# The attention stage of a graph network rewritten: one wide sum per tile, copied out by ScalarE, scaled in place, with rows shared with GpSimd

## The chip, the cores and the metric

One Trainium2 chip, one core of it. The metric is the device time of one execution in microseconds (us), shown as the median of several runs. Engines go by the names of the profile: PE is TensorE, DVE is VectorE, ACT is ScalarE, POOL is GpSimd, SP is SyncE.

## The reference, cut to what matters

The network has 50,000 nodes and 50,000 edges, 64 features, and four layers on a residual stream. The layer that is changed here is the third, a GATv2 attention with 4 heads over the edges and one loop per node:

```python
m = leaky_relu(x_l[src] + x_r[dst] + e_emb, 0.2)
alpha = einsum('ehf,hf->eh', m, att)
amax = segment_max(alpha, dst)
ex = exp(alpha - amax[dst])
denom = segment_sum(ex, dst)
alpha = ex / (denom[dst] + 1e-16)
out = segment_sum(x_l[src] * alpha[..., None], dst).mean(axis=1) + bias
out = gamma * (out - out.mean(axis=0)) * rsqrt(out.var(axis=0) + 1e-5) + beta   # then relu
```

The edges are sorted by `dst`.

## The kernel before, in words

`kernel()` builds a row of stages, each an `nc.Block()` in which every engine has its own instruction list and the engines meet through semaphores alone. In order of time: preparation, two norm layers, the attention's edge scores and segment maximum, the stage `attention("fa")` (line 2465) that is changed, `batch_norm("fb")` (line 2740), three typed layers. A stage starts when the one before has ended on all engines.

**The attention stage** has the scores of every edge and loop ready: the exponentials in the table `exp_all` (8 numbers per edge: 4 exponentials and 4 maxima, one per head), the maxima of the loops in `amax`. It makes the weighted sums of source rows. It goes over the nodes in NS = 56 blocks of HS = 7 tiles of 128 nodes. For a block it loads a window of WT = 8 tiles of edge rows (`win`), their 8 numbers into the last 8 columns of `M`, and the nodes' own rows (`own`). All buffers that matter are double (slot n % 2). Per block, before the change:

- DVE `matrices` (line 2643): one comparison makes `S`, 14 selection matrices of 128x128 (each of the 7 node tiles looks at BAND = 2 edge tiles).
- DVE `messages` (2650): `M[:, :, 0:256]` = edge row times exponential, 4 heads, one instruction of 2048 elements.
- PE `small_sums` (2534): 14 matmuls of 8 columns (sum of exponentials, maximum) into bank 7.
- DVE `differences` and `weights` (2657, 2669): small operations and an exponential by ACT (`exps`, 2596) give two factors per node and head: `cc[:, 0]` for the edges' sum and `cc[:, 1]` for the loop.
- PE `sums` (2545): 14 matmuls of 256 columns, two node tiles to a bank, banks 0 to 3.
- ACT `own_edges` (2600): `mine` = own row times `cc[:, 1]` for 4 of the 7 tiles, 16 instructions. DVE does the other 3 tiles at the top of `scale` (2690).
- DVE `scale` (2690): 28 instructions of 64 columns (tile by head): sum in the bank times `cc[:, 0]` plus `mine`, to `agg`. Each pair of tiles raises `scaled`, which frees its bank.
- PE `turns` (2557): 14 transposes of `agg`; ACT `turned` copies them to `aggT` in 4 pieces; PE `outputs` (2573): the product with the output weights, 64 output partitions, 512 and 384 columns into banks 5 and 6; ACT `outputs` (2617) copies it with the bias to `oT`; SP stores it; DVE `moments` (2679) takes the statistics for the batch norm, two instructions of 448 columns.

The order on PE is sums(n), turns(n-1), small_sums(n+1), outputs(n-1); on DVE matrices(n+1), messages(n+1), moments(n-2), scale(n), differences(n+1), weights(n+1); on ACT own_edges(n), turned(n-1), exps(n+1), outputs(n-1). POOL has nothing in this stage. Each f32 matmul stands in the trace as two weight loads and two matmuls. At the end `bn_aggr` (2726) joins all statistics and a few small operations make the batch norm's factors.

The other lines that the prediction names: 2259, 2260 and 2262 are the sums of the second norm layer, where 2259 writes the bank's partitions 64 to 127 and the other two the partitions 0 to 63; 2783 is a POOL product of the batch norm stage and 2838 a DVE operation beside it; 261 and 1790 are POOL index fills of the preparing stages.

Of the kernel before, what the change touches and what calls it, by code (L numbers as in the profile page):

```python
# [4 lines left out]
P = 128  # L5
F = 64
HEADS = 4
HF = HEADS * F
HS = 7
# [4 lines left out]
WT = HS + 1  # L14
# [4 lines left out]
BAND = 2  # L19
# [8 lines left out]
def build_gnn(nc, a, out):  # L28
# [47 lines left out]
    with ctx:  # L76
# [2388 lines left out]
        def attention(tag):  # L2465
            with nc.cleanup_on_exit(), ExitStack() as c, nc.Block() as block:
# [17 lines left out]
                small = carve(early, [P, HS, E8]); me = carve(early, [P, HS, HEADS]); mm = carve(early, [P, HS, HEADS])  # L2484
# [3 lines left out]
                mine = tb("mine", [P, HS, HEADS, F]); agg = tb("agg", [P, 2, HS, HEADS, F])  # L2488
                aggT = tb("aggT", [P, 2, HS * P]); oT = tb("oT", [F, HS * P])
                stats = tb("stats", [F, 2 * NS, 6]); mv = tb("mv", [F, 4])  # L2490
                win_in, ex_in, own_in = two("win_in"), two("ex_in"), two("own_in")
                (S_ok, M_ok, small_ok, small_read, d_ok, e_ok, c_ok, mine_ok, sums_ok, scaled, aT_made, aT_read, out_made, o_ok, stat_ok, stored, var_ok, sd_ok) = (
                    sm(n) for n in ("S_ok", "M_ok", "small_ok", "small_read", "d_ok", "e_ok", "c_ok", "mine_ok", "sums_ok", "scaled", "aT_made", "aT_read", "out_made",
                                    "o_ok", "stat_ok", "stored", "var_ok", "sd_ok"))
                CH = [(0, 4), (4, HS)]
                PAIRS = [(t, min(t + 2, HS)) for t in range(0, HS, 2)]
                NB = len(PAIRS)
                TURNS = [(0, 0, 4), (0, 1, 5), (1, 0, 6), (1, 1, 4)]
                small_ps = bank[7][:, 0:HS * E8].rearrange("p (t c) -> p t c", c=E8)
                assert N > (NS - 1) * HS * P  # L2500

                @block.sync
                def _(sp):
                    def load(n):
# [3 lines left out]
                        if n >= 2:  # L2508
                            sp.wait_ge(M_ok, n - 1)
                        sp.dma_start(win[:, s, :, :], tiles(edge_all[bass.ds(begin, WR), :])).then_inc(win_in[s], 16)  # L2510
                        if n >= 2:
                            sp.wait_ge(sums_ok, NB * (n - 1))
                        sp.dma_start(M[:, s, :, HF:MW], tiles(exp_all[bass.ds(begin, WR), :])).then_inc(ex_in[s], 16)
                        if n >= 2:
                            sp.wait_ge(scaled, NB * (n - 1))
                        sp.dma_start(own[:, s, :, :], tiles(node_g[at, :])).then_inc(own_in[s], 16)

                    def store(n):
                        sp.wait_ge(o_ok, 2 * n + 2)
                        sp.dma_start(gat_rows[:, n * HS * P:(n + 1) * HS * P], oT[:, :]).then_inc(stored, 16)  # L2520
# [9 lines left out]
                    sp.wait_ge(stored, 16 * NS)  # L2530

                @block.tensor
                def _(pe):
                    def small_sums(n):
                        s = n % 2
                        pe.wait_ge(S_ok, n + 1)
                        pe.wait_ge(ex_in[s], 16 * (n // 2 + 1))
                        if n >= 1:
                            pe.wait_ge(small_read, n)
                        for t in range(HS):  # L2540
                            for q in range(BAND):
                                ins = nc.tensor.matmul(small_ps[:, t, :], S[:, s, BAND * t + q, :], M[:, s, t + q, HF:MW], start=(q == 0), stop=(q == BAND - 1))
                        ins.then_inc(small_ok, 1)

                    def sums(n):
                        s = n % 2
                        pe.wait_ge(M_ok, n + 1)
                        for b, (t0, t1) in enumerate(PAIRS):
                            if n >= 1:
                                pe.wait_ge(scaled, NB * (n - 1) + b + 1)  # L2550
                            for t in range(t0, t1):
                                for q in range(BAND):
                                    ins = nc.tensor.matmul(bank[b][:, (t - t0) * HF:(t - t0 + 1) * HF], S[:, s, BAND * t + q, :], M[:, s, t + q, 0:HF],  # L2553
                                                           start=(q == 0), stop=(q == BAND - 1))
                            ins.then_inc(sums_ok, 1)

                    def turns(n):
                        s = n % 2
                        pe.wait_ge(scaled, NB * (n + 1))
                        for k, (b, q, to) in enumerate(TURNS):  # L2560
                            if k == 3:
                                pe.wait_ge(aT_read, 4 * n + 1)
                            elif n >= 1:
                                if k == 0:
                                    pe.wait_ge(aT_read, 4 * n)
                                else:
                                    pe.wait_ge(o_ok, 2 * (n - 1) + k)
                            t0, t1 = CH[b]
                            for t in range(t0, t1):
                                ins = nc.tensor.transpose(bank[to][:, (t - t0) * P:(t - t0 + 1) * P], agg[:, s, t, 2 * q:2 * q + 2, :].rearrange("p h f -> p (h f)"), ident[:, :])  # L2570
                            ins.then_inc(aT_made, 1)

                    def outputs(n):
                        for b, (t0, t1) in enumerate(CH):
                            pe.wait_ge(aT_read, 4 * n + 2 * b + 2)
                            for q in range(2):
# [350 lines left out]
```

## Time and profile before

| | |
|---|---|
| median of 3 runs | 5102.17 us (5100.82 to 5104.14) |
| the profiled execution's own time | 5098.76 us |
| its span | 5096.6 us |
| PE busy | 4014.7 us (79%) |
| PE weight loads busy | 3596.6 us (71%) |
| DVE busy | 3622.2 us (71%) |
| ACT busy | 2008.4 us (39%) |
| POOL busy | 2562.4 us (50%) |

How to read it: busy times are of the whole span and mix stages with different limits; the attention stage is 2511 to 3341 us. What lies around the span (5098.76 - 5096.6 = 2.2 us) belongs to the launch.

### The profile page before, as it was taken

Reading aid. Unit: us, or ns where it says so; the run is one execution under the profiler, and the core shown is the slowest. Engines: PE = TensorE matmul, PEld = TensorE weight load, DVE = VectorE, ACT = ScalarE, POOL = GpSimd, SP = SyncE. Lnnn points to the kernel's source line nnn. Section 1 sums busy time; section 2 is a strip of 40 time slices with the busy share of each in tenths; the row PEclk is TensorE's granted clock in tenths of the full one; section 3 lists DMA queues with packets and bytes.
Section 4 is the critical chain, followed back from the end, with each engine's and each line's share of the span. In section 5 each row is a group of like instructions: output and inputs, shape, how many; then the busy total and the mean of one; then the engine's idle time right before and its main releaser. Section 6 shows DMA issues by size and latency. Waiting matters only on the chain. (4 is left out here: it accounts for less than half of the span.)

```text
span 5096.6 us, 86759 instructions
## 1 busy us (share of the span) xinstructions
PE 4014.7 (79%) x26962; PEld 3596.6 (71%) x27018; DVE 3622.2 (71%) x9781; ACT 2008.4 (39%) x4938; POOL 2562.4 (50%) x2806
## 2 busy tenths in 40 slices
PE   5710577658887999999399999996888688878888
PEld 5710577658776777777377777786888688877888
DVE  8977577857776999999699999976444344434554
ACT  6836244434444444444154444554222122222222
POOL 0010777747775777776000000035777577757775
PEclk9965777778988999999699999955898888888888
DMA  8013688857775544454122222245666466655665
GB/s 220 6 37 80 144 184 187 189 114 162 160 158 120 119 114 118 115 118 106 32 54 54 52 53 52 52 117 126 133 138 135 105 134 135 137 110 127 136 133 114
DMA packets 1642253, 583.15 MB, mean 114 GB/s; under 512 B 1548519, under 2 KB 1574950, under 8 KB 1641578
## 3 DMA queue, kind: packets, MB, share of 16 engines
q1 hardware_dynamic: 921158, 297.65, 26.1%
q10 hardware_dynamic: 636612, 195.74, 16.5%
q0 software_dynamic: 84064, 84.64, 8.2%
q8 instruction: 205, 3.36, 0.3%
q14 instruction: 214, 1.75, 0.1%
HBM read 381.77 MB, written 209.21 MB: 116 GB/s over the span
## 5 line engine op out<-in xcount | busy, mean ns | idle before, releaser
L2001 POOL DMA_INDIRECT early<-node_g,src_w x1173 | 1115.5, 951 | 427.0 <-issue 356.8
L2218 POOL DMA_INDIRECT early<-node_g,src_w x782 | 758.6, 970 | 297.7 <-issue 249.0
L2783 POOL TENSOR_TENSOR fbt_c<-x_sb,fbln 128x128 f32<-128x128 f32 x56 | 22.4, 400 | 1022.4 <-DVE fbln L2859 1022.4
L1116 POOL DMA_INDIRECT fscat<-node_g,early x392 | 371.7, 948 | 192.9 <-issue 110.5
L2262 PE MATMUL bank<-l0S,l0msg 128*128 128x128 f32 x1568 | 272.6, 353 | 158.0 <-issue 69.2
L1220 ACT ACTIVATE fsy<-bank 128x512 f32<-128x512 f32 x448 | 240.1, 544 | 379.1 <-DVE fslz L1265 201.3
L2262 PEld LDWEIGHTS bank<-l0S,l0msg 128*128 128x128 f32 x1568 | 262.4, 265 | 164.8 <-issue 120.0
L2553 PE MATMUL bank<-early,faS 128*128 128x256 f32 x1568 | 358.0, 386 | 0.0
L2553 PEld LDWEIGHTS bank<-early,faS 128*128 128x128 f32 x1568 | 296.6, 192 | 73.3 <-issue 34.4
L2043 PE MATMUL bank<-l3S,l3msg 128*128 128x128 f32 x1568 | 234.5, 319 | 100.3 <-issue 60.8
L2043 PE MATMUL bank<-l5S,l5msg 128*128 128x128 f32 x1568 | 231.1, 316 | 100.3 <-issue 65.5
L2705 DVE SCALAR_TENSOR_TENSOR faagg<-bank,early,famine 128x64 f32<-128x64 f32 x1568 | 305.7, 275 | 5.7 <-ACT famine L2606 1.6
L2043 PE MATMUL bank<-l4S,l4msg 128*128 128x128 f32 x1568 | 234.6, 320 | 93.0 <-issue 59.3
L2043 PEld LDWEIGHTS bank<-l3S,l3msg 128*128 128x128 f32 x1568 | 225.8, 233 | 104.3 <-issue 104.3
L2043 PEld LDWEIGHTS bank<-l5S,l5msg 128*128 128x128 f32 x1568 | 222.5, 230 | 104.5 <-issue 104.5
L2043 PEld LDWEIGHTS bank<-l4S,l4msg 128*128 128x128 f32 x1568 | 225.8, 233 | 97.1 <-issue 97.1
L1265 DVE TENSOR_TENSOR fslz<-bank,fsy 128x512 f32<-128x512 f32 x448 | 258.3, 618 | 34.2 <-ACT fsy L1220 15.2
L2259 PE MATMUL bank<-ident,l1own 128*64 128x128 f32 x784 | 185.5, 334 | 122.0 <-issue 71.2
L2262 PE MATMUL bank<-l1S,l1msg 128*64 128x128 f32 x1568 | 270.2, 301 | 0.0
L2143 DVE TENSOR_TENSOR l3msg<-early,bank 128x512 f32<-128x512 f32 x112 | 71.9, 684 | 276.3 <-DMA early<-edge_h 276.1
L2143 DVE TENSOR_TENSOR l4msg<-early,bank 128x512 f32<-128x512 f32 x112 | 71.9, 684 | 274.9 <-DMA early<-edge_h 274.8
L1119 POOL DMA_INDIRECT fscat<-node_g,early x224 | 212.4, 948 | 68.3 <-issue 67.4
(365 smaller groups left out, 10920.6 us busy)
## 6 DMA issues: line engine op xcount, KB each, us to landing
edge_h<-early SPq DMA_DIRECT2D x280, 224.0 KB
node_g<-amax ACTq DMA_DIRECT2D x224, 224.0 KB
early<-edge_h SPq DMA_DIRECT2D x168, 256.0 KB
early<-node_g,src_w POOLq DMA_INDIRECT x1955
l0msg<-edge_a ACTq DMA_DIRECT2D x56, 256.0 KB
l0msg<-edge_h SPq DMA_DIRECT2D x56, 256.0 KB
l1msg<-edge_h SPq DMA_DIRECT2D x56, 256.0 KB
alpha<-edge_h SPq DMA_DIRECT2D x56, 256.0 KB
```

What stands on the lines that cost most here:

```text
L1116: pool.indirect_dma_start(out=cat[:, s, t, 0:F], out_offset=None, in_=node_g, in_offset=bass.IndirectOffsetOnAxis(ap=src_i[:, col], axis=0 ...
L1119: pool.indirect_dma_start(out=cat[:, s, t, F:2 * F], out_offset=None, in_=node_g, in_offset=bass.IndirectOffsetOnAxis(ap=dst_i[:, col], ax ...
L1220: A.activation(y[:, g % 2, 0:t1 - t0, :], z_bank(g)[:, 0:(t1 - t0) * HF].rearrange("p (t c) -> p t c", c=HF), ACT.Copy, scale=SLOPE).then_ ...
L1265: v.tensor_tensor(lz[:, kind, t0:t1, :], z_bank(g)[:, 0:(t1 - t0) * HF].rearrange("p (t c) -> p t c", c=HF), y[:, g % 2, 0:t1 - t0, :], AL ...
L2001: pool.indirect_dma_start(out=ring[:, n % RING, t, :], out_offset=None, in_=table_in, in_offset=bass.IndirectOffsetOnAxis(ap=src_w[:, n * ...
L2043: nc.tensor.matmul(to, msg[:, s, t + q, :], S[:, s, BAND * t + q, :], start=(q == 0), stop=(q == BAND - 1))
L2143: ins = v.tensor_tensor(msg[:, n % 2, :, r * F:(r + 1) * F], win[:, n % DEEP, :, :], rel_ps(n)[:, r, :].unsqueeze(2).to_broadcast((P, WT, ...
L2218: pool.indirect_dma_start(out=ring[:, n % RING, t, :], out_offset=None, in_=table_in, in_offset=bass.IndirectOffsetOnAxis(ap=src_w[:, n * ...
L2259: nc.tensor.matmul(bank[2 * s + b][F:2 * F, col], own[:, d, t, :], ident[:, :], start=True, stop=True)
L2262: ins = nc.tensor.matmul(to, msg[:, d, t + q, :], S[:, s, BAND * t + q, :], start=(q == 0 and conv), stop=(q == BAND - 1))
L2553: ins = nc.tensor.matmul(bank[b][:, (t - t0) * HF:(t - t0 + 1) * HF], S[:, s, BAND * t + q, :], M[:, s, t + q, 0:HF], start=(q == 0), stop ...
L2705: ins = v.scalar_tensor_tensor(agg[:, s, t, h, :], bank[b][:, lo:lo + F], cc[:, 0, t, h:h + 1], mine[:, t, h, :], ALU.mult, ALU.add)
```

## The change

All of it is inside `attention`:

- The separate small sums are gone. Each of the 14 matmuls now has 264 columns (256 of messages and 8 of exponentials and maxima). One tile has one bank, tile g uses bank g % 4.
- ACT copies each tile's 264 sums out of its bank into `agg` (`take`, 7 copies per block, semaphore `taken_ok`); a bank is free once its copy is done. `agg` now has 264 columns.
- DVE reads the small sums out of `agg`, waits for all 7 copies before `differences`, and runs `scale` as one in-place instruction of 1792 elements and `add` as two (3 tiles, 4 tiles).
- The own rows: ACT makes 3 tiles (OWN_ACT), POOL 4 in one instruction of 1024 elements. The messages: DVE makes 5 of the 8 edge tiles (MSG_DVE), POOL 3 in one instruction of 768 elements.
- The outputs go to both halves of one bank: columns 0 to 447 to partitions 0 to 63, columns 448 to 895 to partitions 64 to 127. ACT then has one copy per block, DVE one statistics instruction on 128 partitions, and `oT` is double.
- SP stores two halves per block. At the end it moves the upper half's statistics to the lower partitions with a DMA for which `bn_aggr` waits; at the start it loads `shift` (the bias, twice).
- New orders: matrices and messages run two blocks ahead; `outputs` lags two blocks and stands between the sums of tile 3 and tile 4.

The diff, cut to its core:

```diff
-                ACT_TILES = 4
+                OWN_ACT, MSG_DVE = 3, 5
...
                         if n >= 2:
                             sp.wait_ge(M_ok, n - 1)
+                            sp.wait_ge(M2_ok, n - 1)
                         sp.dma_start(win[:, s, :, :], tiles(edge_all[bass.ds(begin, WR), :])).then_inc(win_in[s], 16)
                         if n >= 2:
-                            sp.wait_ge(scaled, NB * (n - 1))
+                            sp.wait_ge(mine_ok, n - 1)
+                            sp.wait_ge(mine2_ok, n - 1)
                         sp.dma_start(own[:, s, :, :], tiles(node_g[at, :])).then_inc(own_in[s], 16)
...
+                    sp.wait_ge(stat_ok, NS)
+                    sp.dma_start(stats[0:F, NS:2 * NS, :], stats[F:2 * F, 0:NS, :]).then_inc(turned_stats, 16)
...
+                @block.gpsimd
+                def _(pool):
+                    def messages(n):
+                        s = n % 2
+                        pool.wait_ge(win_in[s], 16 * (n // 2 + 1))
+                        pool.wait_ge(ex_in[s], 16 * (n // 2 + 1))
+                        k = WT - MSG_DVE
+                        g.tensor_tensor(heads(M[:, s, MSG_DVE:WT, 0:HF]), win[:, s, MSG_DVE:WT, :].unsqueeze(2).to_broadcast((P, k, HEADS, F)),
+                                        M[:, s, MSG_DVE:WT, HF:HF + HEADS].unsqueeze(3).to_broadcast((P, k, HEADS, F)), ALU.mult).then_inc(M2_ok, 1)
+                    def own_edges(n):
+                        s, k = n % 2, HS - OWN_ACT
+                        pool.wait_ge(c_ok, n + 1)
+                        pool.wait_ge(own_in[s], 16 * (n // 2 + 1))
+                        g.tensor_tensor(mine[:, OWN_ACT:HS, :, :], own[:, s, OWN_ACT:HS, :].unsqueeze(2).to_broadcast((P, k, HEADS, F)),
+                                        cc[:, 1, OWN_ACT:HS, :].unsqueeze(3).to_broadcast((P, k, HEADS, F)), ALU.mult).then_inc(mine2_ok, 1)
+                    messages(0)
+                    messages(1)
+                    for n in range(NS):
+                        own_edges(n)
+                        if n + 2 < NS:
+                            messages(n + 2)
...
+                        for t in range(t0, t1):
+                            g = n * HS + t
+                            if g >= 4:
+                                pe.wait_ge(taken_ok, g - 3)
                             for q in range(BAND):
-                                ins = nc.tensor.matmul(small_ps[:, t, :], S[:, s, BAND * t + q, :], M[:, s, t + q, HF:MW], start=(q == 0), stop=(q == BAND - 1))
...
+                                ins = nc.tensor.matmul(bank[g % 4][:, 0:MW], S[:, s, BAND * t + q, :], M[:, s, t + q, :], start=(q == 0), stop=(q == BAND - 1))
...
+                        pe.wait_ge(aT_read, 4 * n + 4)
+                        if n >= 1:
+                            pe.wait_ge(o_ok, n)
+                        for q in range(2):
+                            for half in range(2):
+                                ins = nc.tensor.matmul(bank[7][half * F:(half + 1) * F, 0:HALF], Wst[:, q, :], aggT[:, q, half * HALF:(half + 1) * HALF], start=(q == 0), stop=(q == 1))
...
                     for n in range(NS):
-                        sums(n)
+                        sums(n, 0, SPLIT_AT)
+                        if n >= 2:
+                            outputs(n - 2)
+                        sums(n, SPLIT_AT, HS)
                         if n >= 1:
                             turns(n - 1)
...
+                            A.copy(agg[:, s, t, :], bank[g % 4][:, 0:MW]).then_inc(taken_ok, 1)
...
+                    for n in range(NS):
+                        take(n, 0, 2)
                         if n >= 1:
+                            own_edges(n - 1, 0, 1)
+                        take(n, 2, SPLIT_AT)
                         if n >= 1:
+                            own_edges(n - 1, 1, OWN_ACT)
+                        if n >= 2:
+                            outputs(n - 2)
+                        take(n, SPLIT_AT, HS)
                         if n >= 1:
+                            turned(n - 1, 0, 2)
+                        exps(n)
+                        if n >= 1:
+                            turned(n - 1, 2, 4)
...
                     def differences(n):
-                        dve.wait_ge(small_ok, n + 1)
-                        v.tensor_copy(small[:, :, :], small_ps).then_inc(small_read, 1)
+                        dve.wait_ge(taken_ok, HS * (n + 1))
...
                     def scale(n):
+                        v.tensor_tensor(heads(agg[:, s, :, 0:HF]), heads(agg[:, s, :, 0:HF]), cc[:, 0, :, :].unsqueeze(3).to_broadcast((P, HS, HEADS, F)), ALU.mult)
+                    def add(n):
+                        v.drain()
                         dve.wait_ge(mine_ok, n + 1)
+                        v.tensor_tensor(heads(agg[:, s, 0:OWN_ACT, 0:HF]), heads(agg[:, s, 0:OWN_ACT, 0:HF]), mine[:, 0:OWN_ACT, :, :], ALU.add)
+                        dve.wait_ge(mine2_ok, n + 1)
+                        v.tensor_tensor(heads(agg[:, s, OWN_ACT:HS, 0:HF]), heads(agg[:, s, OWN_ACT:HS, 0:HF]), mine[:, OWN_ACT:HS, :, :], ALU.add).then_inc(agg_ok, 1)
...
                     for n in range(NS):
+                        differences(n)
+                        if n + 2 < NS:
+                            matrices(n + 2)
+                        weights(n)
+                        scale(n)
+                        if n + 2 < NS:
+                            messages(n + 2)
+                        add(n)
                         if n >= 2:
                             moments(n - 2)
...
+                    dve.wait_ge(turned_stats, 16)
```

## Rows read from the trace of the kernel before

**Rows 1.** Stages: stretch, length, busy us of PE, PEld, DVE, ACT, POOL, clock, DMA.

```profile
515.00:1060.00 545.00, 370.43 (x2352) 355.77 (x2352) 401.49 (x1233) 235.43 (x616) 381.12 (x391) 0.75 0.74 172
2522.00:3334.00 812.00, 812.00 (x4342) 621.66 (x4342) 741.52 (x2348) 399.62 (x1287) 0.00 (x0) 0.97 0.26 51
3523.00:4045.00 522.00, 427.81 (x3360) 423.82 (x3360) 220.88 (x284) 113.86 (x224) 370.15 (x391) 0.87 0.58 128
```

**Rows 2.** Timeline: start, duration, engine, line. First and last of 56 `scale` groups on DVE.

```profile
2530.23 5.46 DVE L2705 SCALAR_TENSOR_TENSOR faagg<-bank,early,famine 128x64 f32<-128x64 f32 x28
...
3322.91 5.46 DVE L2705 SCALAR_TENSOR_TENSOR faagg<-bank,early,famine 128x64 f32<-128x64 f32 x28 [1.61 <-ACT famine L2606]
```

**Rows 3.** Timeline of PE over one block at full clock.

```profile
2542.09 1.82 PE L2570 MATMUL bank<-ident,faagg 128*128 128x128 f32 x14
2543.76 3.19 PE L2542 MATMUL bank<-early,faS 128*128 128x8 f32 x28
2546.88 3.22 PE L2577 MATMUL bank<-faaggT,Wst 128*64 128x512 f32 x8
2550.03 6.31 PE L2553 MATMUL bank<-early,faS 128*128 128x256 f32 x28
2556.17 1.82 PE L2570 MATMUL bank<-ident,faagg 128*128 128x128 f32 x14
```

**Rows 4.** Timeline of DVE and ACT over the same block.

```profile
2549.11 0.19 DVE L2662 TENSOR_TENSOR early<-early,no_edge 128x28 f32<-128x28 f32 x1
2549.74 0.18 DVE L2667 TENSOR_TENSOR early<-amax,early 128x28 f32<-128x28 f32 x1
2550.24 0.19 DVE L2671 TENSOR_TENSOR early<-early 128x28 f32<-128x28 f32 x1 [0.32 <-ACT early L2598]
2551.17 0.22 DVE L2677 TENSOR_TENSOR early<-early 128x56 f32<-128x56 f32 x1
2551.30 2.02 DVE L2647 TENSOR_TENSOR faS<-node_id,edge_id 128x1792 f32<-128x1792 f32 x1
2551.42 3.93 ACT L2606 ACTIVATE famine<-early 128x64 f32<-128x64 f32 x16 [0.18 <-DVE early L2677]
2555.44 1.14 DVE L2686 BATCH_NORM_STATS2 fastats<-faoT 64x6 f32<-64x448 f32 x2
2556.81 1.84 ACT L2615 COPY faaggT<-bank 128x512 f32<-128x512 f32 x4 [1.46 <-PE bank L2570]
```

**Rows 5.** Groups by line and shape in the attention stage: busy us, mean ns.

```profile
L2654 DVE TENSOR_TENSOR early<-alpha,early 128x2048 f32<-128x2048 f32 x56 | 127.9, 2284 | 2.8 <-DMA early<-edge_x 2.8
L2615 ACT COPY faaggT<-bank 128x512 f32<-128x512 f32 x112 | 60.2, 590 | 121.0 <-PE bank L2570 121.0
L2694 DVE TENSOR_TENSOR famine<-early 128x768 f32<-128x768 f32 x56 | 53.6, 958 | 9.8 <-issue 9.6
L2615 ACT COPY faaggT<-bank 128x384 f32<-128x384 f32 x112 | 49.3, 503 | 0.0
```

**Rows 6.** Groups of POOL over the whole span, by shape.

```profile
L2783 POOL TENSOR_TENSOR fbt_c<-x_sb,fbln 128x128 f32<-128x128 f32 x56 | 22.4, 400 | 1022.4 <-DVE fbln L2859 1022.4
L1790 POOL IOTA wn_tile_i<- 128x392 int32 x1 | 0.5, 455 | 84.1 <-ACTq L1774 84.1
L261 POOL IOTA row_i<- 128x128 int32 x1 | 0.2, 233 | 0.4 <-POOLq L2912 0.4
```

**Rows 7.** Timeline: DVE and POOL side by side in the batch norm stage.

```profile
3441.37 0.62 DVE L2838 SCALAR_TENSOR_TENSOR x_sb<-bank,x_sb 128x448 f32<-128x448 f32 x1
3441.49 0.40 POOL L2783 TENSOR_TENSOR fbt_c<-x_sb,fbln 128x128 f32<-128x128 f32 x1 [1.36 <-DVE fbln L2859]
```

**Rows 8.** Timeline of PE in the second norm layer, line 2259 of two neighbouring tiles.

```profile
1300.78 0.32 PE L2259 MATMUL bank<-ident,l1own 128*64 128x128 f32 x1
...
1301.43 0.32 PE L2259 MATMUL bank<-ident,l1own 128*64 128x128 f32 x1
```

**Rows 9.** DMA issues within the attention stage: KB each, median us to landing.

```profile
early<-edge_x SPq DMA_DIRECT2D x53, 32.0 KB, 2.2
```

More of the change, by code:

```diff
@@ L2487, in attention @@
                 S = tb("S", [P, 2, BAND * HS, P])
[L2488 to L2494, printed above, removed]
+                agg = tb("agg", [P, 2, HS, MW]); mine = tb("mine", [P, HS, HEADS, F])
@@ new lines, in attention @@
+                HALF = HS * P // 2
+                aggT = tb("aggT", [P, 2, HS * P]); oT = tb("oT", [P, 2, HALF]); shift = tb("shift", [P, 1])
+                stats = tb("stats", [P, 2 * NS, 6]); mv = tb("mv", [F, 4])
+                win_in, ex_in, own_in, stored = two("win_in"), two("ex_in"), two("own_in"), two("stored")
+                (shift_in, S_ok, M_ok, M2_ok, sums_ok, taken_ok, d_ok, e_ok, c_ok, mine_ok, mine2_ok, agg_ok, aT_made, aT_read, out_made, o_ok, stat_ok, turned_stats, var_ok, sd_ok) = (
+                    sm(n) for n in ("shift_in", "S_ok", "M_ok", "M2_ok", "sums_ok", "taken_ok", "d_ok", "e_ok", "c_ok", "mine_ok", "mine2_ok", "agg_ok", "aT_made", "aT_read", "out_made",
+                                    "o_ok", "stat_ok", "turned_stats", "var_ok", "sd_ok"))
@@ L2495, in attention @@
                 CH = [(0, 4), (4, HS)]
[L2496 to L2497 removed]
                 TURNS = [(0, 0, 4), (0, 1, 5), (1, 0, 6), (1, 1, 4)]
[L2499 to L2500 removed]
+                SPLIT_AT = 4
+                last_half = N - (NS - 1) * HS * P - HALF
+                assert 0 < last_half <= HALF
+                heads = lambda ap: ap.rearrange("p t (h f) -> p t h f", h=HEADS)
@@ L2545, in sums @@
[L2545 to L2554, printed above, removed]
+                        if t0 == 0:
+                            pe.wait_ge(S_ok, n + 1)
+                            pe.wait_ge(M_ok, n + 1)
+                            pe.wait_ge(M2_ok, n + 1)
@@ L2571, in turns @@
                             ins.then_inc(aT_made, 1)
                     def outputs(n):
-                        for b, (t0, t1) in enumerate(CH):
-                            pe.wait_ge(aT_read, 4 * n + 2 * b + 2)
-                            for q in range(2):
-                                ins = nc.tensor.matmul(bank[5 + b][0:F, 0:(t1 - t0) * P], Wst[:, q, :], aggT[:, q, t0 * P:t1 * P], start=(q == 0), stop=(q == 1))
-                            ins.then_inc(out_made, 1)
-                    small_sums(0)
+                        pe.wait_ge(aT_read, 4 * n + 4)
@@ L2708, in _ @@
                     matrices(0)
                     messages(0)
-                    differences(0)
-                    weights(0)
+                    matrices(1)
+                    messages(1)
                     for n in range(NS):
-                        if n + 1 < NS:
-                            matrices(n + 1)
-                            messages(n + 1)
+                        differences(n)
[6 more added lines that the diff above has]
+                        add(n)
```

140 lines of the change are left out of this document (61 added, 79 removed).

## The prediction

> **What bounds the kernel now.** I read the stages first [rows 1], the whole time second, the timeline of one block third. The attention stage runs from 2522 to 3334 us with PE busy all the time, DVE 741.5 of 812 us, ACT half, POOL not at all, at a mean clock of 0.97. The change touches this stage alone, so all the rest of the span should stay. The pace of the stage comes from the first and the last `scale` group: they start at 2530.23 and 3322.91, 55 blocks apart [rows 2], which is 792.68 / 55 = 14.41 us per block. Any answer is 55 or 56 times a difference to this number.
>
> Two engines come close to it. PE, from start to start in one block at full clock [rows 3]: transposes 2543.76 - 2542.09 = 1.67, small sums 3.12, outputs 3.15, sums 6.14, together 14.08 us. There is no gap between them, so PE is the limit at full clock; the rest up to 14.41 comes where the clock is lower for a moment. DVE is nearly as full: 741.5 / 812 x 14.41 = 13.2 us busy per block, and its drains fill most of what is left. A change that relieves only one of them wins nearly nothing. This one relieves both.
>
> **PE, part by part.** The small sums cost 3.12 us per block for 8 columns a matmul. They go; the 14 wide matmuls grow from 256 to 264 columns, 6.14 x 264 / 256 = 6.33 us. The transposes stay at 1.67. The outputs have the same columns (2 x 896) but are now pairs, one to each half of the partitions. What this is worth can be read elsewhere in this trace: the norm layer has per tile 4 matmuls of 128 columns in 8 records, two of which (line 2259) go to the upper half [rows 8]. From tile to tile 0.65 us pass (1300.78 to 1301.43). Eight records one after another at the pace of the sums here, 6.14 / 28 = 0.219 us for 256 columns or 0.11 for 128, would need 0.88; six need 0.66. So the upper half's records ran beside the others. I take the outputs at half, 3.15 / 2 = 1.6 us; the other end is 3.15. PE: 6.33 + 1.67 + 1.6 = 9.6 us at full clock, 11.15 if nothing overlaps.
>
> **DVE.** Two-operand operations cost 958 ns for 768 elements and 2284 for 2048 [rows 5], so 1.036 ns per element and 162 fixed. New per block: differences without the copy 2549.92 - 2549.11 = 0.81; matrices 2.02; weights 2551.39 - 2550.24 = 1.15 [rows 4]; scale, 1792 elements as the matrices have, 2.02, in place of 28 instructions in 5.46; messages for 5 tiles, 1280 elements, 1.49 instead of 2.28; add 0.96 (768) and 1.22 (1024); moments one instead of two instructions, 0.6, and its drain and semaphore 0.17. The own rows' 0.96 leave DVE. Sum 10.4; with four or five pauses of about 0.1 at drains and semaphores 10.9 us, against 14.3.
>
> **ACT.** It gets 7 copies of 264 columns. 512 columns take 590 ns and 384 take 503 [rows 5], 0.68 per column, so 0.42 each and 2.9 us. Own rows fall from 16 to 12 instructions of 3.93 / 16 = 0.245, 2.9 us; `turned` stays 1.84 [rows 4]; one output copy 0.6 and an exponential 0.25. Sum 8.6 us. It is not the limit, but its order matters: the own rows of block n wait for `c_ok` and then stand around the copies of tiles 2 and 3 of block n+1. From `c_ok` ACT needs 0.98 + 0.8 + 1.96 = 3.8 us to `mine_ok`; DVE meanwhile does scale and messages, 3.6 us. That wait costs DVE about 0.2. What is queued behind it is `add`, then `turns` on PE. The exponential of block n+1 stands behind two copies of turned rows; those are done 1.9 us after `add(n)`, while DVE is at matrices until 3.7 us. It costs nothing. If that cover went, it would cost 1 us at most.
>
> **POOL.** The nearest row is its product of 128 elements, 400 ns; its index fills give 233 ns for 128 and 455 for 392 elements, so 0.84 per element and 125 fixed [rows 6]. With the same fixed part the product costs (400 - 125) / 128 = 2.15 ns per element: own rows (1024) 2.33 us, messages (768) 1.78 us, sum 4.1 us per block. Bounds: 0.8 (both at 400 ns) and 5.6 (all of the 400 ns by element). The own rows are due when `add` begins its second part, 4.6 us after `c_ok`, the messages one block later: both ends are hidden, if the engines do not disturb each other.
>
> **Do they?** No row shows POOL and DVE in two-operand SBUF work at once. The nearest one has POOL's product inside a DVE operation that reads one operand from a bank; both took their usual 400 and 620 ns [rows 7]. So the disturbance lies between 0 and all of the 4.1 us per block; I take 0, by that row, and keep the other end. The Trainium skill (SBUF — State Buffer, "Who interferes with whom") speaks against it: a VectorE instruction with two SBUF inputs shares its second read path with GpSimd's reads, and the later one is fully blocked until the other has ended. No run here shows that yet; by it the sum would be the slower rival's below.
>
> **SP and the ends.** SP has one more DMA per block (two half stores) and waits for `mine_ok` before it loads own rows, behind which the next window's load stands. That window is issued some 8 us before `messages` needs it; a small load lands in 2.2 us [rows 9]. I cost it at nothing. The ends: the first block now needs its messages before any sum, the last has own rows, add, turns and outputs in a row, and the statistics' DMA is waited for (2.2 us and its issue). Together about 5 us more.
>
> **The sum.** PE 9.6, DVE 10.9 + 0.2: DVE is the limit, 11.1 us. PE is then busy 87% of the time. At 82% (427.8 of 522 us) the typed layer had a mean clock of 0.87 [rows 1], by which PE's 9.6 become 11.0. So I take 11.2 us per block. Saved: 55 x (14.41 - 11.2) = 176.6 us, less 5 for the ends. The profiled execution took 5098.76 us: 5098.8 - 171.6 = 4927.2. The median of the runs is 3.4 us higher: 4930.6, say **4931 us**. With outputs that do not overlap (PE 11.15, at clock 0.97 11.5) it is 4948; with 11.0 us per block 4920.
>
> **Rivals.**
> 1. POOL and DVE exclude each other, in turns (slower). Place: after `c_ok` scale, POOL's own rows, DVE's messages, POOL's messages and add stand in one row. All of DVE's large operations here have two SBUF operands. Price: 10.9 + 4.1 = 15.0 us per block, 0.6 more than now: +33 us, +5 for the ends, 5140 us. It decides from the point where over 14.4 - 10.9 = 3.5 of POOL's 4.1 us are exposed. For it: the rule of the page above; nothing in a row. Against it: rows 7, as far as they reach.
> 2. They exclude each other, but DVE keeps its turn while its instructions follow without a pause, so POOL works in the pauses and beside the moments, which read one operand: some 3.3 us are exposed, 14.2 us per block, 5102.2 - 12 + 5 = 5095 us.
> 3. They slow each other in part, half of POOL's time shows: 13.0 us per block, 5030 us.
> 4. PE goes to its lower clock more often, since it now waits for DVE: at the 0.75 that the norm layer had with 68% busy [rows 1], PE needs 9.6 / 0.75 = 12.8 us, 5019 us. Against it: wide matmuls in a dense row had 0.97 here.
> 5. The change does not do what it says for PE and ACT: the copies hold the four banks so long that PE waits, and ACT's chain (8.6 us and its waits) is the limit, 12 to 13 us, 4980 to 5030. Against it: a tile is summed in 0.9 us and copied in 0.4.
>
> **Chances.** My forecast 0.36; rival 1 0.25; rival 2 0.14; rival 3 0.13; rivals 4 and 5 together 0.12. A measurement of this kernel can tell about 0.2%, 10 us. Faster by more: 0.36 + 0.13 + 0.12 and less than half of rival 2, cut down a little for rival 4 with rival 1's waits, 0.62. Within 0.2%: the rest of rival 2 and the edge of rival 1, 0.10. Slower: 0.28. The range must hold the forecast and, with both signs that likely, reach to rival 1: 4915 to 5142. The forecast's own range is 4915 to 4955.
>
> **What would show it.** In the profile after: 55 blocks in 11.2 us each, read from the starts of `scale`; no 8-column matmuls; the outputs' eight records in about 1.6 us; DVE's scale at 2.02, add 0.96 and 1.22, POOL's products at 2.3 and 1.8 us while DVE's operations run. Right for the forecast is a block in which DVE's large operations keep their length and follow each other although POOL is at work. Wrong is: DVE's or POOL's operations longer than these numbers or with gaps that end when the other engine ends (rivals 1 to 3), PE without gaps and a clock below 0.8 (rival 4), ACT without gaps (rival 5).

## The result, and the profile after

The changed kernel takes 5034.05 us (median of 4 runs, 5026.3 to 5037.59), the kernel before 5101.49 us beside it. The ratio is 0.9866 [0.9854, 0.9879]: 67 us faster, where 171 were forecast. The profiled execution took 5037.59 us, its span 5035.3. Of the profile page of the changed kernel, the first part:

```profile
PE 3799.1 (75%) x25394; PEld 3408.4 (68%) x25450; DVE 3579.0 (71%) x8214; ACT 2050.9 (41%) x5050; POOL 2845.2 (57%) x2918
```

PE lost 216 us of work, POOL gained 283, and DVE, which was to lose some 3 us per block, about 160 in all, lost 43 us in all. So the page's first part already says where to look.

**The pace.** Timeline of the changed kernel, the first and the last of 56 second parts of `add` (they answer to [rows 2]):

```profile
2543.05 1.22 DVE L2745 TENSOR_TENSOR faagg<-faagg,famine 128x1024 f32<-128x1024 f32 x1
...
3261.01 1.22 DVE L2745 TENSOR_TENSOR faagg<-faagg,famine 128x1024 f32<-128x1024 f32 x1
```

717.96 / 55 = 13.05 us per block, against 14.41 before and 11.2 forecast. The 1.85 us above the forecast, 55 times, are 102 of the 110 us by which the profiled execution's time missed it (5037.6 - 4927.2). The same stretch by engines, as in [rows 1]:

```profile
2543.00:3261.00 718.00, 585.10 (x2722) 426.44 (x2722) 677.55 (x765) 431.83 (x1368) 274.82 (x108) 0.93 0.26 56
```

DVE is recorded busy for 678 of 718 us, PE for 585, ACT for 432. DVE is the limit, as forecast; but 677.55 / 718 x 13.05 = 12.3 us of work per block are too much: the sum for DVE's instructions was 10.4.

**Where they are.** Groups of the changed kernel in its attention stage (busy us, mean ns of one | idle time ahead and what ended it; compare [rows 5, 6]):

```profile
L2737 DVE TENSOR_TENSOR faagg<-faagg,early 128x1792 f32<-128x1792 f32 x56 | 211.1, 3770 | 5.1
L2552 POOL TENSOR_TENSOR early<-alpha,early 128x768 f32<-128x768 f32 x56 | 181.6, 3243 | 113.0 <-DMA early<-edge_x 112.9
L2700 DVE TENSOR_TENSOR early<-alpha,early 128x1280 f32<-128x1280 f32 x56 | 153.0, 2733 | 4.9 <-DMA early<-edge_x 4.9
L2633 ACT COPY faagg<-bank 128x264 f32<-128x264 f32 x392 | 143.7, 375 | 139.2 <-PE bank L2582 139.1
L2595 PE MATMUL bank<-ident,faagg 128*128 128x128 f32 x784 | 132.0, 331 | 138.2 <-DVE faagg L2745 138.2
L2559 POOL TENSOR_TENSOR famine<-early 128x1024 f32<-128x1024 f32 x56 | 106.5, 1903 | 452.5 <-DVE early L2722 452.5
L2745 DVE TENSOR_TENSOR faagg<-faagg,famine 128x1024 f32<-128x1024 f32 x56 | 68.2, 1218 | 0.0
L2743 DVE TENSOR_TENSOR faagg<-faagg,famine 128x768 f32<-128x768 f32 x56 | 53.6, 958 | 5.9 <-ACT famine L2642 0.8
```

Two of DVE's instructions are far over their forecast: `scale` takes 3.77 us and not 2.02, `messages` 2.73 and not 1.49. That is 3.0 us per block. There is no gap to find: the idle time ahead of either is nearly nothing, the extra time is inside the instruction's own duration. `add` is on its number, 958 and 1218 ns. PE waits 138 us for DVE's `add`. The timeline of one block of the changed kernel shows why (start, duration):

```profile
2917.18 1.90 POOL L2559 TENSOR_TENSOR famine<-early 128x1024 f32<-128x1024 f32 x1 [8.07 <-DVE early L2722]
2917.20 3.77 DVE L2737 TENSOR_TENSOR faagg<-faagg,early 128x1792 f32<-128x1792 f32 x1
2918.08 1.72 PE L2604 MATMUL bank<-faaggT,Wst 128*64 128x448 f32 x8
2919.05 3.25 POOL L2552 TENSOR_TENSOR early<-alpha,early 128x768 f32<-128x768 f32 x1
2919.73 2.94 PE L2582 MATMUL bank<-early,faS 128*128 128x264 f32 x12
2920.89 2.76 DVE L2700 TENSOR_TENSOR early<-alpha,early 128x1280 f32<-128x1280 f32 x1
2923.74 0.96 DVE L2743 TENSOR_TENSOR faagg<-faagg,famine 128x768 f32<-128x768 f32 x1
2924.61 1.22 DVE L2745 TENSOR_TENSOR faagg<-faagg,famine 128x1024 f32<-128x1024 f32 x1
```

POOL and DVE both start behind the small product that raises the semaphore `c_ok` (L2722), POOL 0.02 us earlier. POOL's product is over at 2919.08; DVE's 2.02 us of scaling would fill 2918.95 to 2920.97. POOL's messages, recorded from 2919.05, end at 2922.30, and DVE's, recorded from 2920.89, end at 2923.65, 1.35 us later. So the four seem to run one after another, each recorded from the moment it was issued; at each hand-over the one that waited ends some 0.13 us sooner than the other's end plus its own full length. That was a reading of one timeline, and two others were open: that they slow each other in proportion (rival 3), or that PE or ACT sets the pace and DVE merely waits. The outputs' eight records take 2919.73 - 2918.08 = 1.65 us, where they took 3.15 [rows 3].

### The profile page after: what moved, and what is told of

Its sections match the earlier page's. It is cut to its first block and busy times, and to the rows that moved or that the text cites. A ratio compares the mean times of both kernels' runs of the same rounds, so it can differ in the third digit from the quotient of the medians.

```text
span 5035.3 us, 82559 instructions
## 1 busy us (share of the span) xinstructions
PE 3799.1 (75%) x25394; PEld 3408.4 (68%) x25450; DVE 3579.0 (71%) x8214; ACT 2050.9 (41%) x5050; POOL 2845.2 (57%) x2918
## 5 line engine op out<-in xcount | busy, mean ns | idle before, releaser
L2582 PE MATMUL bank<-early,faS 128*128 128x264 f32 x1568 | 394.0, 406 | 80.7 <-POOL early L2552 80.4
L2559 POOL TENSOR_TENSOR famine<-early 128x1024 f32<-128x1024 f32 x56 | 106.5, 1903 | 452.5 <-DVE early L2722 452.5
L2552 POOL TENSOR_TENSOR early<-alpha,early 128x768 f32<-128x768 f32 x56 | 181.6, 3243 | 113.0 <-DMA early<-edge_x 112.9
```

Source lines behind the costliest of these rows:

```text
L2552: g.tensor_tensor(heads(M[:, s, MSG_DVE:WT, 0:HF]), win[:, s, MSG_DVE:WT, :].unsqueeze(2).to_broadcast((P, k, HEADS, F)), M[:, s, MSG_DVE: ...
L2582: ins = nc.tensor.matmul(bank[g % 4][:, 0:MW], S[:, s, BAND * t + q, :], M[:, s, t + q, :], start=(q == 0), stop=(q == BAND - 1))
```

## The experiments

The theory: a DVE instruction with two SBUF operands and a POOL instruction that reads SBUF exclude each other for their whole length. The rivals: only part of the time is lost, whichever memory is used; PE's order and clock set the pace; ACT does. "Block" is worked out as above, from the first to the last second part of `add`. Every kernel starts from the changed one; ratios are to the kernel before, timed beside it (5101.49 us for the change; 5098.06, 5097.77 and 5100.16 us in the three sets of experiments). Two rows whose intervals overlap are not told apart by their times alone.

| run | us | ratio | block, us |
|---|---|---|---|
| the change | 5034.05 | 0.9866 [0.9854, 0.9879] | 13.05 |
| write_only | 4865.38 | 0.9544 [0.9525, 0.9563] | 10.17 |
| factors_in_psum | 4886.98 | 0.9583 [0.9567, 0.9599] | 10.46 |
| scale_in_psum | 4933.87 | 0.9682 [0.9666, 0.9698] | 11.34 |
| no_pool | 4974.84 | 0.9763 [0.9746, 0.9779] | 12.04 |
| messages_on_dve | 5002.15 | 0.9811 [0.9795, 0.9828] | 12.59 |
| own_on_dve | 4999.24 | 0.9810 [0.9793, 0.9826] | 12.47 |
| own_after_scale | 5022.14 | 0.9845 [0.9828, 0.9861] | 12.88 |
| outputs_twice | 5037.66 | 0.9888 [0.9871, 0.9904] | 13.10 |
| small_sums_back | 5040.55 | 0.9887 [0.9871, 0.9904] | 13.15 |
| small_sums_back_no_exclusion | 5053.86 | 0.9910 [0.9894, 0.9927] | 13.27 |
| more_on_pool | 4896.07 | 0.9606 [0.9590, 0.9622] | 10.63 |
| own_two_on_act | 4879.66 | 0.9565 [0.9549, 0.9581] | 10.28 |

**write_only.** POOL's two products become fills of the same elements with a constant: POOL still writes, but reads nothing. The weighted messages of 3 edge tiles and the own rows of 4 node tiles are left out of the sums.

```diff
-  g.tensor_tensor(heads(M[:, s, MSG_DVE:WT, 0:HF]), win[...], M[...], ALU.mult).then_inc(M2_ok, 1)
+  g.memset(heads(M[:, s, MSG_DVE:WT, 0:HF]), 0.01).then_inc(M2_ok, 1)
-  g.tensor_tensor(mine[:, OWN_ACT:HS, :, :], own[...], cc[...], ALU.mult).then_inc(mine2_ok, 1)
+  g.memset(mine[:, OWN_ACT:HS, :, :], 0.01).then_inc(mine2_ok, 1)
```

> GpSimd's two products (own rows of 4 tiles, messages of 3 tiles) are replaced by fills of the same regions with a constant; the sums are then of other data. Theory (VectorE instructions with two SBUF operands and GpSimd instructions that read SBUF exclude each other): a fill reads nothing, so VectorE's scale falls from 3.77 to 2.02 us and its messages from 2.75 to 1.49 us; the block falls from 13.05 to about 10.6 us, the time to 4895 to 4925 us. Rival A (every GpSimd instruction in SBUF blocks): scale stays longer than 2.02 us by the length of a fill, about 0.9 us each, time about 4985 us. Rival B (the in-place scale is slow by itself): scale stays 3.77 us, time 5034 us.

Timeline of write_only:

```profile
2756.86 0.96 POOL L2558 MEMSET famine<- 128x1024 f32 x1 [8.53 <-DVE early L2720]
2756.89 2.02 DVE L2735 TENSOR_TENSOR faagg<-faagg,early 128x1792 f32<-128x1792 f32 x1
2757.75 0.74 POOL L2552 MEMSET early<- 128x768 f32 x1
2758.83 1.48 DVE L2698 TENSOR_TENSOR early<-alpha,early 128x1280 f32<-128x1280 f32 x1
```

POOL is at work inside DVE's instruction and DVE's keeps its 2.02 us, then its 1.48. So the in-place `scale` is not slow by itself. The block falls to 10.17 us, 2.88 less than in the change, nearly all of the 3.0, and lower than the 10.6 that were expected. This alone doesn't settle it, since POOL's instructions became shorter too.

**factors_in_psum.** POOL's work stays as it is; of DVE's two large products the small operand (the factors, the exponentials) is read from a bank. Bank 6 holds them, and `turns` makes do with banks 4 and 5.

```diff
-                 TURNS = [(0, 0, 4), (0, 1, 5), (1, 0, 6), (1, 1, 4)]
+                 TURNS = [(0, 0, 4), (0, 1, 5), (1, 0, 4), (1, 1, 5)]
+                 c_ps, e_ps = ...   # two regions of bank[6]
-  v.tensor_tensor(cc[:, :, :, :], d[:, :, :, :], den..., ALU.mult).then_inc(c_ok, 1)
+  v.tensor_tensor(cc[:, 1, :, :], d[:, 1, :, :], den[:, 0, :, :], ALU.mult).then_inc(c_ok, 1)
+  v.tensor_tensor(c_ps, d[:, 0, :, :], den[:, 0, :, :], ALU.mult)
+  v.tensor_copy(e_ps[:, s, :, :], M[:, s, 0:MSG_DVE, HF:HF + HEADS])   # of block n + 2
```

> GpSimd's work stays as it is. VectorE's factor for scale and the factors for its messages lie in a PSUM bank of their own (bank 6, freed by turning through banks 4 and 5 alone), so that scale and messages have one SBUF operand each; one small copy and one small product more per block, 0.3 us. Theory (exclusion of two-operand SBUF work): scale 2.02 us, messages 1.49 us with GpSimd running beside them, 10.5 to 11 us per block, 4895 to 4925 us. Rival A (GpSimd's work slows VectorE whatever its operands are): 3.77 and 2.75 us, 5034 to 5050 us.

Timeline of factors_in_psum:

```profile
2758.92 1.90 POOL L2561 TENSOR_TENSOR famine<-early 128x1024 f32<-128x1024 f32 x1 [7.10 <-DVE early L2728]
2759.10 2.02 DVE L2746 TENSOR_TENSOR faagg<-faagg,bank 128x1792 f32<-128x1792 f32 x1
2760.78 1.47 POOL L2554 TENSOR_TENSOR early<-alpha,early 128x768 f32<-128x768 f32 x1
2761.04 1.48 DVE L2706 TENSOR_TENSOR early<-alpha,bank 128x1280 f32<-128x1280 f32 x1
2762.76 0.96 DVE L2752 TENSOR_TENSOR faagg<-faagg,famine 128x768 f32<-128x768 f32 x1 [0.23 <-ACT famine L2644]
```

The same POOL work, in the same places, now costs DVE nothing, and POOL's messages fall from 3.25 to 1.47 us. The block is 0.29 us above that of write_only. Half of it lies ahead of `scale`, where two small instructions came in: from the product that raises `c_ok` to `scale` 0.45 us pass, and 0.31 in write_only. The other half is DVE's wait for ACT's own rows (0.23, where write_only has a gap of 0.10). This computes the whole reference and is 147 us faster than the change, a little more than expected. A general slowing by POOL's load is out: at equal load, where the operand lies decides. It does not yet tell whether two-operand instructions wait in turns or are slowed in proportion; own_on_dve below does.

**scale_in_psum.** As above for `scale` alone; `messages` still has both operands in SBUF.

```diff
-  v.tensor_tensor(heads(agg...), heads(agg...), cc[:, 0, :, :]..., ALU.mult)
+  v.tensor_tensor(heads(agg...), heads(agg...), c_ps..., ALU.mult)
```

> Half of factors_in_psum: only scale's factor lies in PSUM, the messages keep two SBUF operands. Theory (exclusion, in the order in which they start): scale 2.02 us beside GpSimd's own rows; then GpSimd's messages start 0.1 to 0.3 us before VectorE's, so VectorE's still last 2.75 us. Block 13.05 - 1.75 + 0.1 = 11.4 us, time 5034 - 91 = 4943 us. Rival (the two delays are one and the same, caught up later): about 4887 us or 5034 us.

Timeline of scale_in_psum:

```profile
2754.45 2.02 DVE L2739 TENSOR_TENSOR faagg<-faagg,bank 128x1792 f32<-128x1792 f32 x1
2756.21 1.47 POOL L2553 TENSOR_TENSOR early<-alpha,early 128x768 f32<-128x768 f32 x1
2756.38 2.65 DVE L2701 TENSOR_TENSOR early<-alpha,early 128x1280 f32<-128x1280 f32 x1
```

`scale` is back at 2.02; POOL's messages now come 0.17 us first and keep their 1.47, so DVE's wait: 1.48 + 1.47 - 0.17 = 2.78, recorded 2.65. The one instruction that still has two SBUF operands is the one that is still long, and the block is 11.34 = 10.17 + 1.17.

**no_pool, messages_on_dve, own_on_dve.** DVE does POOL's share: both parts, the messages alone (MSG_DVE = 8), the own rows alone.

```diff
-                OWN_ACT, MSG_DVE = 3, 5
+                OWN_ACT, MSG_DVE = 3, 8        # no_pool, messages_on_dve
+  v.tensor_tensor(mine[:, OWN_ACT:HS, :, :], own[...], cc[:, 1, OWN_ACT:HS, :]..., ALU.mult).then_inc(mine2_ok, 1)   # behind scale: no_pool, own_on_dve
```

> GpSimd does nothing in the stage: VectorE makes all 8 tiles of messages (2.28 us) and 4 tiles of own rows (1.22 us) itself. Theory (exclusion): GpSimd's 1.90 + 1.40 us stood in VectorE's row; without them VectorE has 10.2 - 1.49 + 2.28 + 1.22 = 12.2 us per block, 0.85 less than 13.05, so 4987 us: faster with less help. Rival (GpSimd's help is mostly hidden): VectorE gets 2.0 us more per block, 5034 + 110 = 5144 us.

> VectorE makes all 8 tiles of messages (2.28 us alone), GpSimd only the own rows of 4 tiles. Theory: VectorE's messages go from 2.75 (of which 1.26 us is waiting) to 2.28 us, scale stays at 3.77; block 13.05 - 0.47 = 12.6 us, time 5010 us. Rival (the share of the messages that GpSimd takes is a gain): 0.8 us more per block, 5078 us.

> VectorE makes 4 tiles of own rows itself (1.22 us), GpSimd only the messages of 3 tiles, which now can start before the factors are ready, beside matrices or the small operations. Theory: scale 2.02 instead of 3.77 us, own rows +1.22, and GpSimd's 1.4 us of messages still stand in VectorE's row wherever they fall; block 13.05 - 1.75 + 1.22 = 12.5 us, time 5004 us. If they fall into a time in which VectorE has no two-operand work (moments, reciprocal), up to 1.2 us less. Rival (no exclusion): 1.2 us more per block, 5100 us.

Without POOL, DVE needs 1.22 us for the 4 own rows and 2.28 in place of 1.48 for the messages: 10.17 + 1.22 + 0.80 = 12.19, measured 12.04. That is a whole microsecond below the change, which has help. Each half alone lies between: own rows on POOL cost 1.75 and save 1.22, messages on POOL cost 1.25 and save 0.80. Timeline of own_on_dve, where POOL's messages no longer stand behind its own rows:

```profile
2751.86 2.02 DVE L2685 TENSOR_TENSOR faS<-node_id,edge_id 128x1792 f32<-128x1792 f32 x1
2753.41 1.80 POOL L2552 TENSOR_TENSOR early<-alpha,early 128x768 f32<-128x768 f32 x1 [10.77 <-DMA early<-edge_x]
2753.80 1.45 DVE L2708 TENSOR_TENSOR early<-faagg,early 128x28 f32<-128x28 f32 x1
```

POOL's is issued during `matrices`, which keeps its 2.02; POOL waits for its end (1.80 us in place of 1.47) and then holds up an instruction of 28 elements: 1.45 us in place of 0.18. So DVE keeps its turn too, if it came first, and the wait does not depend on the size of the one that waits. A slowing in proportion can't make 1.45 us of 0.18; a turn that has to be waited out does. With this, rival 3 is out as a mechanism. (The exponentials' product is the usual case in this run: the median of its 56 instructions is 1455 ns, the shortest took 179.)

**own_after_scale.** POOL's own rows wait for the end of `scale` and not for `c_ok`.

```diff
-                        pool.wait_ge(c_ok, n + 1)
+                        pool.wait_ge(sc_ok, n + 1)
-  v.tensor_tensor(heads(agg...), heads(agg...), cc[:, 0, :, :]..., ALU.mult)
+  v.tensor_tensor(heads(agg...), heads(agg...), cc[:, 0, :, :]..., ALU.mult).then_inc(sc_ok, 1)
```

> The changed kernel, but GpSimd's own rows wait until scale is done, so that VectorE starts first. Theory (whichever has started keeps the other out until it ends): scale takes 2.02 us; VectorE's messages have started before GpSimd's own rows and take 1.49 us; GpSimd's own rows (1.90) and messages (1.4) then stand in front of add's first and second part, 2.9 and 2.6 us instead of 0.96 and 1.22. The wait moves and does not shrink: block 13.1 to 13.4 us, time 5034 to 5055 us. Rival (only the order at scale costs time): scale and messages at full speed and add unhindered, about 4890 us.

Timeline of own_after_scale:

```profile
2758.99 1.48 DVE L2700 TENSOR_TENSOR early<-alpha,early 128x1280 f32<-128x1280 f32 x1
2759.15 3.08 POOL L2559 TENSOR_TENSOR famine<-early 128x1024 f32<-128x1024 f32 x1 [7.73 <-DVE faagg L2737]
2760.56 2.48 DVE L2743 TENSOR_TENSOR faagg<-faagg,famine 128x768 f32<-128x768 f32 x1
2762.19 2.18 POOL L2552 TENSOR_TENSOR early<-alpha,early 128x768 f32<-128x768 f32 x1
2762.97 2.49 DVE L2745 TENSOR_TENSOR faagg<-faagg,famine 128x1024 f32<-128x1024 f32 x1
```

`scale` and `messages` are short again, but the two parts of `add`, until now on their number, take 2.48 and 2.49 us: 2.8 us more, in place of 3.0. In 13 of the 31 blocks between 2600 and 3000 us the first part looks otherwise:

```profile
2619.49 1.01 DVE L2743 TENSOR_TENSOR faagg<-faagg,famine 128x768 f32<-128x768 f32 x1 [1.56 <-ACT famine L2642]
```

There DVE waits for ACT's own rows, comes later and finds POOL nearly done: 1.56 + 1.01 us, in place of 2.48 and the usual gap of 0.1, so the sum is the same. The wait moved and hardly shrank. The block is 12.88 us, below the 13.1 to 13.4 expected and 0.17 below the change; that is 9 of the 12 us between the two times, whose intervals overlap. This run answers one more rival, that the two engines collide because they use the same buffer: the second part of `add` reads and writes `agg` and reads `mine` (`faagg`, `famine`), POOL's messages beside it use neither, and it still takes 2.49 us.

**outputs_twice, small_sums_back.** PE's side. The first makes each output product twice, the second puts the 14 small sums back, into columns of the banks that nothing reads.

```diff
-                        for q in range(2):
+                        for q in (0, 1, 0, 1):
```

```diff
+  nc.tensor.matmul(bank[g % 4][:, MW + E8:MW + 2 * E8], S[:, s, BAND * t + q, :], M[:, s, t + q, HF:MW], start=(q == 0), stop=(q == BAND - 1))
```

> The output products of each block are made twice over, 1.7 us more on TensorE per block. Theory (VectorE with GpSimd's work in its row sets the pace, TensorE waits 1.9 to 3.2 us per block for add): the time stays within 10 us of 5034 us. Rival (TensorE at its granted clock of 0.93 is as much the limit): up to 55 x 1.7 = 94 us more, 5100 us or above.

> The changed kernel with the 14 eight-column matmuls of each block made again, into unused columns of each tile's bank (the result is not used): one large part of the change undone on TensorE, 3.1 us per block. Theory (VectorE with GpSimd's work in its row sets the pace of 13.05 us, TensorE needs 9.7 at full clock): TensorE comes to 12.8 us, just below the pace; the time rises by 0 to 30 us over 5034. Rival (the removal of the small sums is what the change won): 3.1 x 55 = 170 us more.

Windows of the stage's middle, the change, outputs_twice and small_sums_back:

```profile
2600.00:3000.00 400.00, 324.67 (x1508) 236.94 (x1506) 378.98 (x423) 237.96 (x756) 156.80 (x62) 0.93 0.27 57
```

```profile
2600.00:3000.00 400.00, 349.45 (x1760) 233.72 (x1757) 379.15 (x422) 243.54 (x761) 156.99 (x62) 1.00 0.29 58
```

```profile
2600.00:3000.00 400.00, 396.94 (x2366) 310.90 (x2365) 378.84 (x426) 243.01 (x758) 155.36 (x62) 1.00 0.26 58
```

DVE is at 379 of 400 us in all three. PE takes on 25 and then 72 us of records, and the blocks grow by 0.05 and 0.10 us, some 3 and 6 us in all. The times are 3.6 and 6.5 us higher, their ratios by 0.0022 and 0.0021 with overlapping intervals, so no growth beyond some 10 us is there. PE is not the limit of the change, and the removal of its small sums is worth next to nothing in it.

**small_sums_back_no_exclusion.** The same matmuls in factors_in_psum.

```diff
+  nc.tensor.matmul(bank[g % 4][:, MW + E8:MW + 2 * E8], S[:, s, BAND * t + q, :], M[:, s, t + q, HF:MW], start=(q == 0), stop=(q == BAND - 1))
```

> The same matmuls put back into factors_in_psum. Theory: there TensorE's 9.7 us were near VectorE's 10.46, so TensorE at 12.8 us becomes the limit: 55 x 2.3 = 128 us more than 4887, 5015 us. Together with small_sums_back this tells when the removal of TensorE's work counts.

Window of small_sums_back_no_exclusion:

```profile
2600.00:3000.00 400.00, 392.82 (x2336) 309.10 (x2338) 289.35 (x480) 245.52 (x747) 99.97 (x60) 1.00 0.26 58
```

Here DVE has 111 us free of 400 and PE 7: 167 us more than factors_in_psum, of which the block accounts for 55 x (13.27 - 10.46) = 155. So PE's part of the change is worth much, but only once DVE is out of POOL's way. With both in place one hides the other. The expectation of 128 us was too low by 39. The window accounts for most of it: PE is busy 392.82 / 400 x 13.27 = 13.0 us per block, where 12.8 were taken, and idle for another 0.24. What is left, 12 us, lies outside the 55 blocks and stays open.

**more_on_pool, own_two_on_act.** Which share is best in factors_in_psum.

```diff
-                OWN_ACT, MSG_DVE = 3, 5
+                OWN_ACT, MSG_DVE = 3, 3        # more_on_pool
+                OWN_ACT, MSG_DVE = 2, 5        # own_two_on_act
```

> factors_in_psum with the messages shared the other way: VectorE 3 tiles (0.96 us), GpSimd 5 tiles (1280 elements, about 2.4 us). Theory: without exclusion a share moved to GpSimd is a gain as far as TensorE lets it: VectorE 10.46 - 0.5 = 9.9 us, TensorE 9.7 to 10.0 us at full clock; block 10.0 to 10.2 us, time 4865 to 4880 us. If GpSimd's longer work now meets add (two SBUF operands), add waits up to 0.7 us and the gain is gone: 4887 us or above.

> factors_in_psum with one more tile of own rows on GpSimd (ScalarE 2, GpSimd 5 tiles). Theory: ScalarE's own rows end 1 us earlier, VectorE's wait of 0.2 us for them goes; GpSimd's messages end 0.4 us later and meet add's first part (now 2 tiles), which has two SBUF operands: 0.2 to 0.4 us of waiting. Block 10.3 to 10.6 us, time 4878 to 4893 us, no difference that counts.

Timeline of more_on_pool:

```profile
2757.64 2.33 POOL L2554 TENSOR_TENSOR early<-alpha,early 128x1280 f32<-128x1280 f32 x1
2757.89 0.95 DVE L2706 TENSOR_TENSOR early<-alpha,bank 128x768 f32<-128x768 f32 x1
2759.62 1.17 DVE L2752 TENSOR_TENSOR faagg<-faagg,famine 128x768 f32<-128x768 f32 x1 [0.78 <-ACT famine L2644]
```

A miss: 4896 us where 4865 to 4880 were expected, 9 more than factors_in_psum and 0.17 us more per block. DVE's shorter messages only bring it earlier to ACT's own rows, for which it waits 0.78, and then `add`, which has two SBUF operands, begins inside POOL's longer product and loses another 0.2. Taking a row from ACT removes the wait for ACT: 4879.66 us, 154 below the change and 220 below the kernel before in the same set. Of the versions that compute the reference it has the lowest time, though its interval overlaps that of factors_in_psum, as expected.

## Why the prediction was wrong

**The step that failed** is "I take 0, by that row". Rows 7 have POOL's product inside a DVE instruction, both at their usual length; but that DVE instruction reads one operand from a bank. Every large DVE instruction of the changed stage reads two from SBUF. The prediction saw that difference ("reads one operand from a bank") and still let the nearest row decide between 0 and 4.1. factors_in_psum shows that this is the very difference on which the cost hangs. The bound "all of the 4.1" was right in kind: nearly all of POOL's time was exposed, only POOL's time is 1.90 + 1.47 = 3.37 us, and 3.0 of it show; the rest is POOL's lead of 0.02 and the 0.13 us saved at each of three hand-overs. The Trainium skill (SBUF — State Buffer, "Who interferes with whom") has the rule: a VectorE instruction with two SBUF inputs contends with a GpSimd instruction that reads SBUF, not with one that only writes. The runs agree on both halves: 3.77 against 2.02 us, and 2.02 beside a fill.

**The rivals.** Rival 1, in turns, is the mechanism, with a price that was too high: 10.9 + 4.1 = 15.0 forecast, 10.17 + 2.88 = 13.05 measured. Two terms were too large. DVE undisturbed needs 10.17 us per block (write_only) and not 10.9: `differences` and `weights` had been taken from start to end, with their pauses in, and 0.5 us of pauses were added once more, while large instructions that follow each other overlap in the records (`scale` lasts 2.02 and `messages` starts 1.94 behind it). POOL needs 1903 ns for 1024 elements and 1474 for 768, 1.68 ns per element and about 0.19 us fixed, and not the 2.15 that were drawn from one row of 128 elements [rows 6]; by these two figures that row comes out right too, at 405 ns for 400, so it was the fixed part, borrowed from the index fills, that was too small. So it came out faster than before and not slower, 1.36 us per block below 14.41. Rival 2, that DVE keeps its turn as long as its instructions follow each other, is wrong: POOL gets in between two of them in every block. Rival 3 has the right time, 13.0 and 5030, and the wrong reason, which is luck: its half was picked between two ends, and own_on_dve's 1.45 us for an instruction of 0.18 is a turn waited out, not a slowing in part.

**The forecast itself** would have missed even with a disturbance of 0: the versions without it run in 10.17 to 10.46 us per block and 4865 to 4887 us, below the forecast's own range of 4915 to 4955. Its 11.2 came mostly from the pauses counted twice, and in part from a granted clock of 0.87 taken over from the typed layer; in write_only it was 1.00.

**PE.** Window and timeline of write_only:

```profile
2600.00:3000.00 400.00, 391.05 (x1968) 279.31 (x1969) 372.18 (x552) 305.68 (x981) 63.84 (x78) 1.00 0.35 75
```

```profile
2599.98 1.88 PE L2593 MATMUL bank<-ident,faagg 128*128 128x128 f32 x14 [0.20 <-DVE faagg L2743]
2601.70 3.73 PE L2580 MATMUL bank<-early,faS 128*128 128x264 f32 x16
2605.36 1.72 PE L2602 MATMUL bank<-faaggT,Wst 128*64 128x448 f32 x8
2607.01 2.94 PE L2580 MATMUL bank<-early,faS 128*128 128x264 f32 x12
```

From start to start the transposes take 1.72 us (1.67 forecast), the outputs 1.65 (1.6), the sums 3.66 and the 2.94 of the last record, 6.6 in all (6.33): 9.97 us where 9.6 were forecast. PE waits only 0.20 us per block for `add`, so it stands right behind DVE. Rival 4 is out: the granted clock was 0.93 over the stage of the change, and 1.00 in the stage's middle in small_sums_back at nearly the same time. The clock did fall for moments: in the change, behind a wait of 3.22 us for `add`, it was 0.60 from 2925.80 to 2929.00, and the 14 transposes took 2.78 us in place of 1.88. But that is time of PE's, which had it to spare.

**ACT.** The copies take 375 ns, 0.42 were forecast, and ACT is busy 432 of 718 us. Rival 5 is out for the change; in factors_in_psum DVE does wait 0.23 us per block for ACT's own rows, the 0.2 that the prediction had.

**The ends.** The start grew by 7.2 us (from the stage's first instruction to the end of the first block's `scale` or `add`) and the tail by 2.7, together 9.9 for the 5 of the sum. In the changed kernel the timeline of the tail has the wait for the statistics' DMA:

```profile
3270.55 0.59 SPq L2539 DMA_DIRECT2D fastats<-fastats  x1
3272.67 3.18 DVE L2765 BATCH_NORM_AGGREGATE famv<-fastats 64x2 f32<-64x672 f32 x1 [2.17 <-DMA fastats<-fastats]
```

It is the 2.2 us that [rows 9] gave. The start came to 7.2, but mostly not as an error of its own: in write_only it grew by 2.2 us only and the tail by 1.9, together 4.1 for the 5. The rest comes with POOL's products (the start of factors_in_psum, which has them, grew by 4.7).

**Left open.** How the 67 us of the change divide between PE's and DVE's parts on their own was not tried: no run has the old outputs with the new DVE order.

## What to carry to other kernels

Before work is given to GpSimd, list which VectorE instructions it will run beside and where each reads its operands: where both of its operands lie in SBUF and GpSimd reads too, the help was paid for at nearly full length, and here doing it all on VectorE was 59 us faster than sharing. Moving the small broadcast operands to a bank cost one copy of 0.17 us and one small product per block, and brought 147 us. And when the nearest row differs from the new case in the one thing on which a known rule turns, the row is no evidence against the rule.

## What the runs showed that was not expected

- The wait for the other engine is recorded inside the duration of the instruction that waits, with no idle time and no releaser ahead of it. A group's mean that grew (2022 to 3770 ns at the same shape) is the only sign, and an instruction of 28 elements can show 1455 in place of 179 ns.
- Neither engine has a right of way: in the change POOL led by 0.02 us and DVE waited; in own_on_dve and own_after_scale DVE led and POOL waited (1.80 for 1.47, 3.08 for 1.90).
- The exclusion moves with the order and does not go away: 3.0 us per block at `scale` and `messages` in the change; in own_after_scale 2.8 at `add`, in some blocks partly as a wait for ACT.
- POOL's fill of 1024 elements took 956 ns and of 768 elements 738 ns, half of the products of the same size (1903 and 1474).
